# A graph layer with residual layer norm on one core: row statistics in interleaved pairs, splits in halves of a period, the message weight folded into W and b

## The reference

```python
messages = einsum('ei,oi->eo', x[dst], W) + b
out      = segment_sum(messages * agg_weight, src, num_segments=N)
h        = x + out
result   = (h - mean(h)) / sqrt(var(h) + 1e-5)      # over the 128 features of a row
```

## Time and profile before

| what | us |
|---|---|
| median of 3 runs | 1273.84 |
| lowest and highest run | 1270.81, 1276.02 |
| span of the profiled execution, first to last instruction | 898.2 |
| that execution's own time | not recorded |
| busy: PE, DVE | 735.0, 853.2 |
| busy: ACT, POOL | 656.6, 592.8 |
| first gather starts, last gather starts | 245.2, 855.5 |

### The profile page before, as it was taken

The page is one execution under the profiler, slowest core; times in us unless marked ns, Lnnn a source line. Parts: engine busy times, 40 slices in busy tenths (PEclk is TensorE's granted clock), DMA queues, the critical chain, the costliest instruction groups (busy, mean ns, idle before and its releaser), DMA issues.

```text
span 898.2 us, 24417 instructions
## 1 busy us (share of the span) xinstructions
PE 735.0 (82%) x7822; PEld 549.6 (61%) x7849; DVE 853.2 (95%) x3877; ACT 656.6 (73%) x1690; POOL 592.8 (66%) x601
## 2 busy tenths in 40 slices
PE   4889999999978778787877887879778787797874
PEld 3735555555456666666766676657666666675664
DVE  7989999999959999999999999999999999999997
ACT  2157777777526777777887778777777787878778
POOL 3047777776477777777777777776777777777710
PEclk9999999999999999989999999998999989989898
DMA  2001111110225677676666766676666666666653
GB/s 74 24 15 38 38 38 38 38 38 26 87 82 166 206 217 213 213 220 215 212 215 207 212 210 212 208 215 204 205 209 217 210 211 206 215 208 211 210 182 120
DMA packets 81035, 141.18 MB, mean 157 GB/s; under 512 B 19360, under 2 KB 20396, under 8 KB 80908
## 3 DMA queue, kind: packets, MB, share of 16 engines
q1 hardware_dynamic: 62476, 110.55, 36.7%
q0 software_dynamic: 18432, 29.08, 13.4%
HBM read 87.64 MB, written 51.92 MB: 155 GB/s over the span
## 4 chain that ended last, share of the span: by engine, by line
DVE 66%; PE 22%; issue 7%; ACT 2%; POOL 2%; DMA 0%; SPq 0%; ACTq 0%; DVEq 0%; POOLq 0%
DVE stats L997 16%; DVE h L991 11%; DVE sel L982 10%; PE bank L648 9%; DVE rest L980 8%; DVE xl L985 7%; DVE mv L1003 7%; PE bank L542 2%; PE bank L597 2%; PE bank L726 2%; PE bank L603 2%; ACT y L1107 1%; POOL xg L516 1%; PE bank L612 1%; DVE rstd L1007 1%
## 5 line engine op out<-in xcount | busy, mean ns | idle before, releaser
L516 POOL DMA_INDIRECT xg<-in_x,now x441 | 448.7, 1018 | 173.1 <-issue 132.5
L1107 ACT ACTIVATE y<-h,shift,rstd 128x128 f32<-128x128 f32 x784 | 320.2, 479 | 0.1
L726 PE MATMUL bank<-wT,aggT 128*128 128x128 f32 x1568 | 242.2, 301 | 0.0
L726 PEld LDWEIGHTS bank<-wT,aggT 128*128 128x128 f32 x1568 | 203.4, 203 | 28.4 <-issue 11.9
L696 PE MATMUL bank<-sel,xg 128*128 128x308 bf16 (+11 forms) x685 | 170.3, 261 | 7.6 <-DVE xl L985 7.6
L698 PE MATMUL bank<-sel,rest 128*128 128x308 bf16 (+11 forms) x685 | 176.4, 261 | 0.0
L479 POOL DMA_INDIRECT place_scratch<-word_col,place_row x135 | 135.7, 1005 | 55.4 <-issue 50.1
L997 DVE BATCH_NORM_STATS2 stats<-h 128x6 f32<-128x128 f32 x784 | 168.9, 275 | 0.2
L700 PE MATMUL bank<-sel,xl 128*128 128x308 bf16 (+11 forms) x685 | 166.9, 261 | 0.0
L1101 ACT ACTIVATE std<-mv,eps 128x4 f32<-128x4 f32 x196 | 58.3, 298 | 131.0 <-DVE mv L1003 130.9
L991 DVE SCALAR_TENSOR_TENSOR h<-bank,aw,xt 128x512 f32<-128x512 f32 x196 | 145.5, 742 | 6.3 <-PE bank L726 5.4
(11 more groups left out here) (153 smaller groups left out, 938.3 us busy)
## 6 DMA issues: line engine op xcount, KB each, us to landing
xt<-in_x SPq DMA_DIRECT2D x195, 256.0 KB, 3.8
out<-y SPq DMA_DIRECT2D x195, 256.0 KB, 2.6
xg<-in_x,now POOLq DMA_INDIRECT x441, 3.8
hi_row<-hi_scratch SPq DMA_DIRECT2D x50, 128.0 KB
place_scratch<-word_col,place_row POOLq DMA_INDIRECT x135
place_scratch<-scattered SPq DMA_DIRECT2D x1, 441.0 KB, 3.6
scattered<-place_scratch SPq DMA_DIRECT2D x1, 441.0 KB, 3.2
src_rows<-in_src SPq DMA_DIRECT2D x1, 192.0 KB
```

The costliest lines, as they stand in the source:

```text
L516: nc.gpsimd.indirect_dma_start(out=xg[:, m, k], out_offset=None, in_=x, in_offset=bass.IndirectOffsetOnAxis(ap=now[:, m, k, 0:1], axis=0)) ...
L726: last = nc.tensor.matmul(OUT[u % RO][:, nodes[j]], aggT[:, u % RO, nodes[j]], wT[:], start=False, stop=True, skip_group_check=True)
L1107: nc.scalar.activation(y[:, u, j], h[:, u, j], ACT.Identity, bias=shift[:, u, j:j + 1], scale=rstd[:, u, j:j + 1]).then_inc(s_y, 1)
```

## The change

It has six parts.

1. **Statistics.** One `bn_stats` takes two rows interleaved (element 0 of the one, element 0 of the other, and so on), so that its "even" and "odd" results are the two rows' own mean and sum of squared deviations. `bn_aggr` and `mv` go; the root takes sum / 128 + eps.
2. **Roots per two groups.** Root, reciprocal and shift run once per pair of groups, on eight columns. `normalise` lags by five rounds instead of four.
3. **Splits in halves.** `select` works on a half period, lists 0 to 4 and then 5 to 8, and stands behind every second `add_x`.
4. **Straight from the table.** `now` and its copies go. Gathers and `sel` read `table`. POOL itself waits for the ring of `xg` to come free (`s_agg`).
5. **Weight folded.** W is scaled by the weight when ACT copies `wT`, and b on DVE before its split, so `add_x` is a plain sum of two tensors.
6. **Semaphores** follow: one per ring place and half for the gathers.

```diff
@@ -36,7 +36,7 @@
     TAIL_FROM = SPAN_N - LISTS * TAIL
-    CLASS = [[k for k in range(LISTS) if max(FIRST[k] - TAIL, 0) // GN == u] for u in range(SPAN_G)]
+    HALVES = [[k for k in range(LISTS) if max(FIRST[k] - TAIL, 0) // GN // 2 == half] for half in range(2)]
     PARTS = []
@@ -194,13 +194,11 @@
         deg = sb("deg", [P, 2, GN], bf16)
-        stats = sb("stats", [P, R, 4, 6])
-        mv = sb("mv", [P, R, 4, 2])
+        stats = sb("stats", [P, R, 4, 3])
         std = sb("std", [P, R, 4])
...
-        baw = sb("baw", [P, D])
         xg1 = sb("xg1", [P, D])
@@ -508,17 +503,21 @@
-                def gather(g, u, n, period, m, mn):
-                    if u % SPAN_G == 0:
-                        pool.wait_ge(s_idx, period + 1)
+                def gather(period, m):
+                    pool.wait_ge(s_idx, 1 if period < RX else 2)
+                    pool.nop(nofuse=True)
+                    if period >= RX:
+                        pool.wait_ge(s_agg, (period - RX + 1) * SPAN_G)
                         pool.nop(nofuse=True)
-                    for k in CLASS[u % SPAN_G]:
-                        nc.gpsimd.indirect_dma_start(
-                            out=xg[:, m, k], out_offset=None, in_=x,
-                            in_offset=bass.IndirectOffsetOnAxis(ap=now[:, m, k, 0:1], axis=0)
-                            ).then_inc(s_rest[m][u % SPAN_G] if k else s_first[m], 16)
-
-                rounds([(gather, 0)])
+                    for half in range(2):
+                        for k in HALVES[half]:
+                            nc.gpsimd.indirect_dma_start(
+                                out=xg[:, m, k], out_offset=None, in_=x,
+                                in_offset=bass.IndirectOffsetOnAxis(ap=table[:, period * LISTS + k, 0:1], axis=0)
+                                ).then_inc(s_rows_in[m][half], 16)
+
+                for period in range(PERIODS):
+                    gather(period, period % RX)
@@ -683,13 +682,9 @@
                     q = u % 2
-                    pe.wait_ge(s_lower, min(g + 2, GA) if u % SPAN_G == SPAN_G - 1 else g + 1)
-                    if u % SPAN_G < SPAN_G - 1:
-                        pe.wait_ge(s_sel, LISTS * period + sum(len(c) for c in CLASS[:u % SPAN_G + 1]))
-                    elif last_group:
-                        pe.wait_ge(s_sel, LISTS * period + LISTS)
-                    else:
-                        pe.wait_ge(s_sel, LISTS * period + LISTS + 1)
+                    halves_in = 2 * period + (1, 1, 2, 2 if last_group else 3)[u % SPAN_G]
+                    pe.wait_ge(s_lower, halves_in)
+                    pe.wait_ge(s_sel, halves_in // 2 * LISTS + halves_in % 2 * len(HALVES[0]))
                     lists = lists_of(g)
@@ -814,8 +809,9 @@
             V.tensor_scalar(most_wide[:], ones[0:HI], most_hi[:], None, ALU.mult).then_inc(s_mx, 1)
-            after(V.tensor_copy(b_parts[:, 0], b_bc[:]))
-            after(V.tensor_tensor(b_res[:], b_bc[:], b_parts[:, 0], ALU.subtract))
+            after(V.tensor_scalar(baw[:], b_bc[:], aw[:], None, ALU.mult))
+            after(V.tensor_copy(b_parts[:, 0], baw[:]))
+            after(V.tensor_tensor(b_res[:], baw[:], b_parts[:, 0], ALU.subtract))
             after(V.tensor_copy(b_parts[:, 1], b_res[:]))
@@ -900,15 +896,13 @@
                 after(V.tensor_scalar(tabq[:, c], i2[:, c], (GN - 1) << 16, 16, AND, LSR))
-                after(V.tensor_tensor(table[:, c, 1], tabq[:, c], emp[:, c], OR))
+                return V.tensor_tensor(table[:, c, 1], tabq[:, c], emp[:, c], OR)
...
             head = LISTS * RX
-            decode(0, head)
+            decode(0, head).then_inc(s_idx, 1)
...
                 dve.wait_ge(z_init, 4)
-                V.tensor_scalar(baw[:], b_bc[:], aw[:], None, ALU.mult).then_inc(z_baw, 1)
-                dve.wait_ge(z_baw, 1)
                 with dve.Fori(0, C) as c:
@@ -956,76 +950,62 @@
             with dve.Else():
-                for period in range(RX):
-                    V.tensor_copy(now[:, period].rearrange("p k w -> p (k w)"),
-                                  table[:, period * LISTS:period * LISTS + LISTS].rearrange("p k w -> p (k w)")).then_inc(s_idx, 1)
-                decode(head, NB)
-
-                def fetch(g, u, n, period, m, mn):
-
-                    if u % SPAN_G == 0 and not (g < RX * SPAN_G):
-                        at_least(dve, s_agg, g - (RX - 1) * SPAN_G)
-                        V.tensor_copy(now[:, m].rearrange("p k w -> p (k w)"),
-                                      table[:, bass.ds(period * LISTS, LISTS)].rearrange("p k w -> p (k w)")
-                                      ).then_inc(s_idx, 1)
-
-                def select(g, u, n, period, m, mn):
-                    dve.wait_ge(s_idx, period + 1)
-                    at_least(dve, s_agg, g - (SPAN_G + 2))
-                    mine = CLASS[u % SPAN_G]
+                decode(head, NB).then_inc(s_idx, 1)
+
+                def select(half_no):
+
+                    period, half = half_no // 2, half_no % 2
+                    m, mn = period % RX, period // RX
+                    mine = HALVES[half]
                     lists = slice(mine[0], mine[-1] + 1)
-                    if u % SPAN_G == 0:
-                        dve.wait_ge(s_first[m], 16 * mn + 16)
-                    dve.wait_ge(s_rest[m][u % SPAN_G], (16 * mn + 16) * len([k for k in mine if k]))
+                    at_least(dve, s_agg, 2 * half_no - 4)
+                    dve.wait_ge(s_rows_in[m][half], (16 * mn + 16) * len(mine))
                     V.tensor_tensor(rest[:, m % 2, lists], xg[:, m, lists], top[:, m, lists, :, 1], ALU.subtract).then_inc(s_upper, 1)
+                    dve.wait_ge(s_idx, 1 if period < RX else 2)
                     for k in mine:
                         V.tensor_scalar(sel[:, m % 2, k, 0:WIDTH[k]], iota_win[:, WIN[k]:WIN[k] + WIDTH[k]],
-                                        now[:, m, k, 1:2], None, ALU.is_equal).then_inc(s_sel, 1)
-                    dve.wait_ge(s_upper, g + 1)
+                                        table[:, period * LISTS + k, 1:2], None, ALU.is_equal).then_inc(s_sel, 1)
+                    dve.wait_ge(s_upper, half_no + 1)
                     V.tensor_tensor(xl[:, m % 2, lists], rest[:, m % 2, lists], middle[:, m % 2, lists, :, 1], ALU.subtract).then_inc(s_lower, 1)
...
                     at_least(dve, s_y, 4 * g - 4 * R + 4)
-                    V.scalar_tensor_tensor(h[:, u].rearrange("p j d -> p (j d)"), OUT[u % RO][:], aw[:],
-                                           xt[:, u].rearrange("p j d -> p (j d)"), ALU.mult, ALU.add).then_inc(s_h, 1)
+                    V.tensor_tensor(h[:, u].rearrange("p j d -> p (j d)"), OUT[u % RO][:],
+                                    xt[:, u].rearrange("p j d -> p (j d)"), ALU.add).then_inc(s_h, 1)
...
                 def moments(g, u, n, period, m, mn):
+
                     dve.wait_ge(s_h, g + 1)
-                    for j in range(4):
-                        V.bn_stats(stats[:, u, j], h[:, u, j]).then_inc(s_stats, 1)
-
-                def combine(g, u, n, period, m, mn):
-                    dve.wait_ge(s_stats, 4 * g + 4)
-                    dve.nop(nofuse=True)
-                    for j in range(4):
-                        V.bn_aggr(mv[:, u, j], stats[:, u, j]).then_inc(s_mv, 1)
+                    for j in range(0, 4, 2):
+                        V.bn_stats(stats[:, u, j:j + 2].rearrange("p two f -> p (two f)"),
+                                   h[:, u, j:j + 2].rearrange("p two d -> p d two")).then_inc(s_stats, 1)
...
                 def invert(g, u, n, period, m, mn):
-                    dve.wait_ge(s_std, g + 1)
-                    V.reciprocal(rstd[:, u], std[:, u]).then_inc(s_rstd, 1)
+                    if u % 2:
+                        dve.wait_ge(s_std, g // 2 + 1)
+                        V.reciprocal(rstd[:, u - 1:u + 1], std[:, u - 1:u + 1]).then_inc(s_rstd, 1)
...
                 def recentre(g, u, n, period, m, mn):
-                    dve.wait_ge(s_rstd, 2 * g + 1)
-                    V.scalar_tensor_tensor(shift[:, u], mv[:, u, :, 0], -1.0, rstd[:, u], ALU.mult, ALU.mult
-                                           ).then_inc(s_rstd, 1)
+                    if u % 2:
+                        dve.wait_ge(s_rstd, g // 2 * 2 + 1)
+                        V.scalar_tensor_tensor(shift[:, u - 1:u + 1], stats[:, u - 1:u + 1, :, 1], -1.0, rstd[:, u - 1:u + 1],
+                                               ALU.mult, ALU.mult).then_inc(s_rstd, 1)
...
-                lead = lambda g: min(6, 4 + g // 4)
-                for g in range(lead(0)):
-                    one(select, g)
+                after_add = {g: g // 2 + 3 for g in range(2, 4 * PERIODS, 2) if g // 2 + 3 < 2 * PERIODS} | {0: 2, 1: 3}
+                select(0)
+                select(1)
                 for g in range(GA + 1):
-                    one(fetch, g + 13)
                     one(add_x, g)
```

(17 more changed lines are left out.)

9 lines of the change are left out of this document (3 added, 6 removed).

## The result

| what | us |
|---|---|
| change, median of 5 runs (lowest, highest) | 1306.39 (1296.77, 1335.48) |
| before, median of 5 runs beside it | 1273.84 (1270.81, 1282.24) |
| ratio, 95% interval | 1.0223, 1.017 to 1.0276 |
| profiled execution of the change: time, span | 1335.48, 1333.8 |

The account below looks back on a forecast made before the run. DVE bounds the kernel now, and POOL would after the change. 244.8 us to the first gather, 553 of gather steps, 39 of collisions and 28.5 of end give 865.4; plus 375.6 makes 1241 us, range 1221 to 1266.

Parts of the forecast that it names:

- the sum: Whole kernel: start, gather steps, collisions and end give 865.4 us of span; 375.6 us carried over unchanged gives 1241 us.
- the new wait on `s_agg`: POOL's wait for the group twelve back, passed by PE two to three halves earlier: priced at zero.
- The bound: Main loop: POOL sets the pace at 12.1 us per period, above DVE's 10.6, PE's 10.5 and ACT's 9.4.
- Stretching: POOL's gathers lengthened when they start during DVE's `rest` or `xl`: 0.80 us per period, 39 us in all.
- rival 2: Main loop: POOL and DVE fall into a rhythm with fewer collisions; without any, 1202 us; chance 5%.
- 88% busy: DVE between 300 and 800 us: falls to about 88% busy, its idle time ended by landings ahead of `rest`.
- Statistics: DVE's two instructions of 256 interleaved elements per group: 0.33 us each, 2.6 us per period.
- Rivals 3 and 4: DVE's interleaved statistics read runs at half rate (7%, 1255 us) or a third or worse (5%, 1363 us).
- rival 5: Main loop: a ring through ACT and PE, 10.7 us per four groups, decides if PE's queue adds 2; 1262 to 1277; 7%.
- Runs of `sel`: DVE's unbroken runs of five and four `sel` could cost POOL about 0.3 us more per period, 15 us in all.
- Start and end: Ahead of the first gather 0.4 us saved; from the last gather's start to the end 28.5 us instead of 42.7.
- its sign: Timed runs: the change is faster, 1241 us against 1273.84; faster had a chance of 0.85.

Follow-up runs that it names:

- e9: The kernel before, unchanged, run for its trace in executions with late PE results: 1281.72 us, ratio 1.0016 to the before beside it.
- b0: The kernel before, unchanged, one run for a trace, without late PE results: 896.79 us.
- a0: The changed kernel, unchanged, one run on the same chip as b0, without late PE results: 846.83 us, ratio 0.944.
- e13: The changed kernel with POOL's wait ahead of its gather burst set two groups later: 1232.61 us, ratio 0.9845 to before.
- e16: The kernel before with DVE's copy `now`, which lets the gather burst go, two groups sooner: 1290.49 us, ratio 1.0252 to before.
- e4: The changed kernel without the ninth gather of each period, 392 gathers instead of 441: 793.72 us, ratio 0.8846 to before.
- e6: The kernel before with 40 dummy products on PE ahead of every fourth group: 1354.61 us, ratio 1.0825 to before.
- e11: The changed kernel with gathers for the first four periods only, later periods reusing their rows: 934.94 us, ratio 0.7434 to before.
- e10: The changed kernel without PE's third product of each list, with late PE results: 1171.78 us, ratio 0.9093 to before.
- e8: The changed kernel with three dummy products on PE ahead of every group: 1396.42 us, ratio 1.0943 to before.
- e7: The changed kernel with 40 dummy products on PE ahead of every fourth group: 1373.4 us, ratio 1.0996 to before.

## Why the prediction was wrong

**The step that failed** is the one in the sum: "Nothing in the change touches what lies around the span except some thousand fewer instructions, so I carry 375.6 over". Next to nothing lies around the span (1.7 to 2.9 us in the runs here). The 376 us were inside before's timed runs. e9's trace, 388 us longer than b0's, has about 127 of them in the sort and 255 in the loop (first gather at 368.0, not 240.5; 17.7 us per period, not 12.48). I had a profile of one kind of execution and times of another, noted the gap and gave it a harmless place. It made every term after it a statement on the wrong bound: in those runs POOL waits for PE, and most of PE's late results come only behind the end of POOL's burst.

**The mechanism that decided** was in no rival. I had priced the new wait on `s_agg` "at zero", because PE had passed it two to three halves earlier. So it is when results come in time: a0 has no such wait. In the other executions POOL waited 364.8 us there, 45 times. The old copy `now` stood on DVE behind the addition of a group; it let the burst go later than the ring required. After a late result, before reached its next burst in 4.6 us (807.49 to 812.1), the change in 7.1 (794.54 to 801.7), since there the last of four groups must be aggregated first (4.6 and 7.1 are also the medians of 36 and 37 such places). With 11.1 to 11.6 us of burst and 1.6 to 1.8 to the release this makes 17.8 and 20.0 us. Burst to burst, the means are 18.0 and 19.3; in the change 40 of 44 steps take 18.2 to 20.1 us and four 15.0 to 16.1.

e13 and e16 move only the start of the burst, in opposite directions, and each turns the sign. That the place of the burst made the change slower is shown by e13, which has all the rest of the change. The 7.1 us go with it, since they shrink to 2.7 there; e16 loses by another path, which was not followed. Why PE's results wait at all is not shown.

**The terms that can be read from a0**, where the model applies:

- *The bound*: POOL, right. The period was 11.7 us, not 12.1; first to last gather 573.6 us, not 592.
- *Stretching*: the mis-sized term, part of the way to rival 2. 440.4 − 441 × 0.952 = 20.6 us, 0.42 per period, where I took 0.80 from a random phase. DVE now waits for a landing ahead of `rest`, 44 times in 98, so the phase is not random; that this made the difference was not tested.
- *DVE*: I forecast 88% busy; 452.60 of 500 is 91%. Statistics 0.33 us for 256 interleaved elements, as forecast. Rivals 3 and 4 are out, and e4, which runs below 800, puts out the ring of rival 5. The Trainium skill (SBUF — State Buffer, the note on cachelines under Door 1) says that an access which crosses to a new line pays a penalty. The read whose elements are 512 bytes apart shows none here: 0.33 us for its 256 elements against 0.195 for 128 in a row.
- *Runs of `sel`*: the mean gather fell from 1021 ns in b0 to 999 in a0, with unbroken runs of five and four `sel`. The Trainium skill (SBUF — State Buffer, section SBUF: two separate sides) says that a `tensor_scalar` in a two-port mode locks GpSimd out of writing descriptors. The prediction's estimate from that, 15 us, shows in no run here; whether `sel` is in such a mode wasn't tested.
- *Start and end*: first gather 241.6 against 240.5 in b0, so the 0.4 us cannot be seen; last gather to end 29.9, forecast 28.5.

Together the change saves 50 us of 897 where I had 33. The forecast was for the timed runs, so that its sign holds in these executions does not make it right.

## What to carry to other kernels

If the profiled span and the timed runs disagree, no model of the span may be carried to the runs: settle first what the runs do, by a profile whose own time is known. A wait that costs nothing under one bound has to be priced under the others too, above all where it decides when a long burst on one queue begins. Here, in the executions with late results, letting the burst go later took 3.7% off the change (0.9845 against 1.0223 of before), and letting it go in two pieces 13.5% (0.884); the whole change gains 5.6% in the others. Neither was run in those others, where POOL has no such wait.

## What the runs showed of the hardware

- One program has two kinds of execution on one core: 898 and 1254 us on chip 12, at different times. In the longer one, PE's results come up to 9.8 us after their modelled end (e9, from the first burst of nine on). The sort has such waits too: ACT waited 55.0 us, 35 times, for a product of PE that had long ended by the records of the change's profile. What brings it on stays open. So does what holds the sort back: it issues 135 indirect DMAs of its own, and no run took them away.
- In the loop such a result is released 1.0 to 2.0 us after the end of an unbroken run of indirect gathers, for runs of 8 and 9 in eight kernels (307 of 419 late ones; e6 has only one late result and isn't among them). A run of 36 at the loop's start goes with results up to 37 us late. Whether it is the issue of the gathers or their transfers that counts was not separated: e11 took both away.
- With late results, a ninth less work on PE (e10) gained 11% (0.9093 of before against the change's 1.0223), where without them it gained nothing. More of it (e8, 1.0943), though only zeros, cost 7%.
- A granted clock of 1.00 does not do away with late results: 40 dummy products in a row (e7) and 12 spread out (e8) ran at 1.00 and 0.83 from 600 to 800 us, and 45 results were late in each. The two took 1.0996 and 1.0943 of the before beside them, so they can't be told apart by time.
